# Reordering the weight-slice hand-over of an attention kernel: later key halves on ScalarE and VectorE, and a moved loop boundary on TensorE

## The reference

```python
x = x + attention(layernorm(x), Wq, bq, Wk, bk, Wv, bv)
x = x + (layernorm(x) @ (weight * scale_weight[:, None]).T + bias)

def attention(h, ...):
    q, k, v = split_heads(h @ W + b)            # each (n, 16, 1024, 64)
    ctx = local_attention(q, k, v)              # block of 128 queries, keys i*128-64 .. (i+1)*128+64
    idx = [0] + top_62_by_norm(q) + [1023]      # 64 tokens of each head
    g = softmax(q[idx] @ k.T / 8) @ v           # these see all keys
    ctx[idx] = g                                # and overwrite the local result
    return merge_heads(ctx)
```

## Time and profile before

| | value |
|---|---|
| median of 3 runs | 2297.66 us |
| the profiled execution | 2297.34 us |
| its span in the trace | 2295.7 us |
| PE busy | 2193.9 us (96%) |
| DVE busy | 1528.1 us (67%) |
| ACT busy | 861.1 us (38%) |
| POOL busy | 598.9 us (26%) |
| the chain that ended last | PE 75%, DVE 15%, issue 5% |
| mean granted TensorE clock | 0.986 |

### The profile page before, as it was taken

One profiled execution on the slowest core, in us unless ns is written; L12 is line 12 of the kernel. 1 busy time (PEld: TensorE's weight loads), 2 busy tenths in 40 slices (PEclk: granted clock), 3 DMA queues, 4 the chain that ended last, 5 costly groups with the idle time before them and its releaser, 6 DMA issues.

```text
span 2295.7 us, 40806 instructions
## 1 busy us (share of the span) xinstructions
PE 2193.9 (96%) x13024; PEld 1866.5 (81%) x13024; DVE 1528.1 (67%) x3434; ACT 861.1 (38%) x2218; POOL 598.9 (26%) x464
## 2 busy tenths in 40 slices
PE   5999999989999999899999998999999977999999
PEld 4878888878788888787888887878888866888887
DVE  6687775665877756648777556486775566666664
ACT  2334445542254455432544555325445550000000
POOL 1332222124322231243212312432123103222211
PEclk9999999999999999999999999999999988999999
DMA  3321111103211111032111110321111103333331
GB/s 129 100 69 51 39 58 41 51 29 109 76 44 47 57 41 50 28 109 75 41 50 57 41 50 28 109 74 42 50 57 39 32 26 128 130 137 137 137 128 73
DMA packets 106170, 159.13 MB, mean 69 GB/s; under 512 B 9616, under 2 KB 75222, under 8 KB 106064
## 3 DMA queue, kind: packets, MB, share of 16 engines
q1 hardware_dynamic: 98128, 138.98, 18.8%
q10 hardware_dynamic: 4608, 16.78, 1.8%
q0 software_dynamic: 3328, 2.17, 0.5%
HBM read 106.48 MB, written 51.41 MB: 69 GB/s over the span
## 4 chain that ended last, share of the span: by engine, by line
PE 75%; DVE 15%; issue 5%; POOL 1%; ACT 1%; DMA 1%; DVEq 0%; SPq 0%; POOLq 0%; ACTq 0%
PE proj L460 33%; PE proj L748 15%; PE pv L596 8%; PE turn L586 5%; PE score L571 4%; PE pv L640 2%; DVE x_norm L1154 2%; PE score L621 2%; DVE top_idx L1152 2%; DVE top_val L1150 2%; PE turn L739 1%; PE misc L508 1%; PE misc L608 1%; DVE q_sq L1117 1%; DVE norms L1119 1%
## 5 line engine op out<-in xcount | busy, mean ns | idle before, releaser
L460 PE MATMUL proj<-xT_hi,w_hi 128*128 128x512 f32 x1536 | 401.7, 403 | 11.3 <-DVE kT_lo L1135 6.5
L460 PE MATMUL proj<-xT_hi,w_lo 128*128 128x512 f32 x1536 | 409.9, 398 | 0.4 <-issue 0.4
L460 PE MATMUL proj<-xT_lo,w_hi 128*128 128x512 f32 x1536 | 382.1, 391 | 0.0
L460 PEld LDWEIGHTS proj<-xT_lo,w_hi 128*128 128x128 f32 x1536 | 288.5, 188 | 63.4
L460 PEld LDWEIGHTS proj<-xT_hi,w_lo 128*128 128x128 f32 x1536 | 281.4, 189 | 62.8 <-issue 1.0
L460 PEld LDWEIGHTS proj<-xT_hi,w_hi 128*128 128x128 f32 x1536 | 275.3, 189 | 68.2 <-DVE kT_lo L1135 8.2
L870 ACT ACTIVATE probs<-score,neg_max 128x256 f32<-128x256 f32 (+1 forms) x512 | 229.2, 460 | 182.2 <-DVE neg_max L1199 97.7
L354 POOL TENSOR_TENSOR ctx_out<-pv_sum,row_inv 128x256 f32<-128x256 f32 x128 | 82.0, 641 | 709.8 <-DVE pv_sum L1236 704.6
L330 POOL CAST w_hi<-w_raw 128x1024 fp32r<-128x1024 f32 x96 | 114.9, 1197 | 520.9 <-PE proj L460 397.1
L332 POOL TENSOR_TENSOR w_lo<-w_raw,w_hi 128x1024 fp32r<-128x1024 f32 x96 | 236.5, 2463 | 7.8
L596 PE MATMUL pv<-v_nat,pT_lo 128*128 128x128 f32 x1024 | 199.4, 276 | 0.0
(11 more groups left out here) (147 smaller groups left out, 3629.3 us busy)
## 6 DMA issues: line engine op xcount, KB each, us to landing
w_raw<-in_wstream SPq DMA_DIRECT2D x96, 512.0 KB, 4.1
q_store<-in_rows SPq DMA_DIRECT2D x72, 512.0 KB, 3.4
q_rows<-q_nat SPq DMA_DIRECT2D x64, 256.0 KB
ctx_rows<-ctx_out SPq DMA_DIRECT2D x128, 128.0 KB, 1.8
q_store<-ctx_rows SPq DMA_DIRECT2D x32, 512.0 KB, 4.1
out<-q_store ACTq DMA_DIRECT2D x32, 512.0 KB, 2.6
bias_b<-in_bias_ffn SPq DMA_DIRECT2D x1, 512.0 KB, 7.6
idx_cols<-idx_dram POOLq DMA_DIRECT2D x32, 1.0 KB, 2.5
```

Source lines behind the costliest of these rows:

```text
L460: mm = pe.matmul(proj[:, bank, :], w[b][:, k * P:k * P + P], x[:, k, half * HALF:half * HALF + HALF], start=(m == 0), stop=(m == 23), skip ...
```

## The change

Four things are edited; no instruction that computes is added or removed.

1. PE: head(n) and rest(n) become one function batch(n). The order of the matmuls and transposes stays, but the loop's boundary moves from behind the first key slices of the next batch to the end of attend. PE's wait for norm_rows_set before the first scores goes.
2. ACT, unit: k_hi_out of the first half moves behind the global exponentials and pv_lo, and its wait for scored goes.
3. ACT, opening: norms_out(n, 1) moves ahead of k_hi_out(n, 0, 0).
4. DVE, unit: row_moments takes the place of k_lo_out of the first half; top_norms(5) moves ahead of split_q; k_lo_out of the first half comes behind split_q.

```diff
-            def head(n):
+            def batch(n, following):
                 turn_early_q(n, 0, 0)
                 turn_early_q(n, 0, 1)
                 project_half(n, 2, 0, (0,))
                 turn_early_q(n, 1, 0)
                 project_half(n, 2, 0, (1,))
-
-            def rest(n, following):
                 turn_early_q(n, 1, 1)
 ...
-                pe.wait_ge(norm_rows_set, n * 2 + 2)
-                apart(pe)
                 with pe.Fori(0, PAIRS - 1) as hp:
 ...
-            head(0)
             with pe.Fori(0, BATCH - 1) as n:
-                rest(n, True)
-                head(n + 1)
-            rest(BATCH - 1, False)
+                batch(n, True)
+            batch(BATCH - 1, False)
@@ ACT, attend
-                if not last:
-                    act.wait_ge(scored, u * EVENTS + EVENTS)
-                    out(1, 0)
                 global_exps(u)
                 pv_lo_out(u, 3)
+                if not last:
+                    out(1, 0)
@@ ACT, batch
+                norms_out(n, 1)
                 k_hi_out(n, 0, 0)
-                norms_out(n, 1)
@@ DVE, attend
                 global_maxima(u)
                 if not last:
-                    k_lo_out(n, hp + 1, 0)
+                    row_moments(n, hp + 1, tile)
                 pv_sums(u, 3)
+                top_norms(5)
                 if not last:
                     split_q(u + 1, hp + 1)
-                    row_moments(n, hp + 1, tile)
-                top_norms(5)
+                    k_lo_out(n, hp + 1, 0)
```

## The result

The changed kernel takes 2350.01 us (median of 4, 2348.29 to 2351.74) beside 2298.65 for the kernel before; ratio 1.0222, 95% interval 1.0205 to 1.0238. The forecast was 2330, its range ended at 2348: the direction was right, 32.5 us were forecast and 51.4 came. The profiled execution took 2351.89 us with a span of 2350.3, 54.6 more than before.

A forecast was written before the change was run, and what follows sets the result against it. TensorE was taken as the bound, busy 2193.9 of 2295.7 us, so its new waits count in full. Terms +14.6, +21.4, -9.6, +4.8 and +1.3 gave +32.5 us: 2330 us, 1.4% slower, range 2312 to 2348.

The forecast's parts named there:

- Ordinary units: Units hp 0, 1, 2, 4, 5 of each batch: PE waits 0.73 us for the later kT_lo, 20 times, +14.6 us.
- Unit 3: Its tail: search and top_rows ahead of kT_lo make PE wait 7.5 us and the clock fall; +21.4 us over four batches.
- The old waits: PE's waits at unit 3's end and in unit 4 (1.58, 1.14, 0.95, on average 0.65 us) all go.
- the hold-off: Unit 3's tail: POOL's w_hi and w_lo hold off DVE's conversions, so the list ends 1.7 us later.
- Opening: Each batch's start: kT_lo 1.6 us later behind norms_out, batch 0 absorbing its own; +4.8 us, clock fall not priced.
- Loop boundary: Batch loop's branch at its new place: still 3.9 us, PE idle 2.2 instead of 1.5 us, twice; +1.3 us.
- Units 6 and 7: Unit 7's v_nat wait falls from 4.28 to about 2.8 us and the clock falls less often; -9.6 us.
- Rival B: Clock decides: it also falls in the openings (+8.8) and still in unit 7 (+6); +47, 2345 us, chance 0.24.
- A: Rival: POOL does not hold top_rows off, unit 3 costs 4.2 us in all; +15.3, 2313 us, chance 0.22.
- C: Rival: faster, no new wait in 20 units; -3.5, or -21 (2276 us) with unit 3's old waits gone; chance 0.03.
- D: Rival: nothing changes for PE because the copy's bank is free earlier in another way; 2298 us, chance 0.03.

The follow-up runs named there:

- e9: e3 with VectorE's k_lo_out moved ahead of split_q: 2312.65 us, 1.0079 against the kernel before.
- e5: Changed kernel with GpSimd's value split of unit 3 held until top_rows is done: 2339.26 us, 1.0187 against the kernel before.
- e2: Kernel before with only ScalarE's opening edit, norms_out(n, 1) ahead of k_hi_out(n, 0, 0): 2305.01 us, 1.0036.
- e1: Kernel before with only TensorE's batch loop end moved behind the last unit, the wait on norm_rows_set kept: 2302.24 us, 1.0029.
- e8: Kernel before with unit 6's row_moments and row_roots moved from its tail to mid-unit: 2281.61 us, 0.9938.
- e11: e8 plus, in unit 7, the third part of v_nat ahead of row 6 on ScalarE and VectorE: 2263.65 us, 0.9865.
- e3: Kernel before with both unit edits (ScalarE and VectorE), but top_norms(5) left behind the kT_lo copy: 2306.08 us, 1.0042.
- e4: Kernel before with both unit edits whole (ScalarE and VectorE), opening and TensorE's loop as before: 2331.23 us, 1.0148.

## Why the prediction was right in its direction and wrong in size

The two traces differ by 54.6 us where 32.5 were forecast. Of the 22 us between, the openings make 7.5, units 6 and 7 make 6.6, the loop's boundary 5.7, and the rest 2.3. In two of the three the length of the wait was nearly right and the clock behind it was priced wrongly.

**Ordinary units: right.** 0.73 forecast, 0.76 measured; e9 shows that the query halves ahead of the copy are what costs it, and not ScalarE's later kT_hi, which e9 has as well.

**Unit 3: right.** 7.5 us forecast and 6.81 seen; the clock fell to 0.63 to 0.72 in all four. The old waits went, but for 0.27 to 0.69 us for v_nat in unit 4 of three batches, where none was forecast. e5 shows the hold-off. The search's last step and the first conversion slipped in before POOL as forecast.

**Opening: the step that failed most.** It was priced as three waits of 1.6 us, "the clock may fall, which I leave to a rival". Behind all four the clock fell in the changed kernel (0.79, 0.78, 0.76, 0.60; e2: three of four). The waits were 3.04 to 3.26, as good as the forecast's 3.1 to 3.3. Batch 0 absorbed most of its own, as forecast, since its waits for w_lo went: 1.1 us. Batches 1 to 3 took 3.5, 3.6 and 4.1 instead of 1.6 each, so 12.3 in all instead of 4.8. The row used against it, 1.76 us with a full clock, was far below the wait forecast, while one of 3.52 us with a fall was in the table; the nearer row should have decided.

**Loop boundary: failed.** The branch was taken to cost the 3.9 us of its old place; it costs 5.0 to 5.8 in the new one. The forecast's own sum with these gives 0.3 + 5.8 + 0.3 - 2.3 = 4.1 and 0.3 + 5.0 + 0.3 - 2.3 = 3.3, beside the 3.97 and 3.22 seen, and the clock falls to 0.76 behind both: 7.0 instead of 1.3. e1 shows it alone. Why the branch costs more there is open.

**Units 6 and 7: mis-sized.** The wait fell from 4.28 to 3.09 us in batches 0 to 2 (2.8 forecast), but the clock still fell behind it, to 0.76 in all three; in batch 3 two waits of 1.94 and 1.12 us took its place, with 0.88 behind the first. The forecast had put 1.5 us of clock per batch on the gain's side. e8 and e11 show that the clock falls behind a second wait of 3.1 us too, and that it stays when that wait is 0.55. So -3.0 came instead of -9.6. The kernel before had a sign of it that the forecast did not use: behind the second wait of unit 7, of 1.69 us, the clock is 0.76 in batches 0 and 1.

Rival B, with 47 us, had the openings and unit 7 right and was the nearest, but it had the boundary at 1.3 us as well; weighing it at 0.24, below the forecast, was the error. What a row shows after 3.5 us in one place was to be expected after 3.1 to 3.3 in another. A is refuted by e5 and by the 6.81 us, C and D by the first row of the waits.

## What to carry to other kernels

Where TensorE is 96% busy, price a new idle time of about 3 us or more at its length and 1.5 to 3 us again for the clock, at every place where it stands. Here the clock fell behind 10 of 12 openings' waits of 3.0 to 3.3 us (changed kernel, e2, e5) and behind 9 of 12 of unit 7's of 3.1 us (changed kernel, e3, e4, e5); the price is an expectation and not a certainty. Where VectorE and GpSimd run side by side, a VectorE chain late by half a microsecond can cost two, since even a tiny instruction may be held behind a copy of 2.4 us: look at what starts just before what, and move work into idle time in mid-unit and not behind it. A wait that is removed uncovers the next one, so list the second before pricing the first.

## What was not expected of the hardware

The taken branch of one and the same loop on TensorE's sequencer took from 3.34 to 5.79 us by where the loop's end was written, while that of the batch loop on the other engines took 0.05 to 0.07. And the granted clock is not a function of the last idle time alone: openings' waits of 3.26 us (e2, batch 3) and 3.12 us (e5, batch 0) and unit 7's of 3.09 us (e4, twice; e5, once) were followed by 1.00. The other way, 1.69 us in unit 7 of the kernel before was followed by 0.76 in two batches and by 1.00 in the third, and openings' waits of 1.76 (e8, batch 3) and 1.77 us (e11, batch 2) by 0.76 where the same wait elsewhere kept 1.00. No run here shows what decides between them.
